# A mixture-of-experts feed-forward in two parts: tokens by chunk, then tiles of one expert pair

## The chip, the cores and the metric

The kernel runs on one core of one Trainium2 chip. The metric is the device time of one execution in microseconds (us).

## What is computed

One layer over 4 batches of 1024 tokens with 256 features (4096 tokens). `xn` is the layer norm of the input, and the output is the input plus a causal attention of `xn` plus a block of 16-head attention and feed-forward. The feed-forward, cut to what matters:

```
x = _rmsnorm(src + sa, norm1_w)
flat = x.reshape(S, C)
shared = _swiglu(flat @ W_shared_in) @ W_shared_out
g_probs = jax.nn.softmax(flat @ Wg_gate + group_bias, -1)
g_idx = jnp.argmax(g_probs, axis=-1)
...
topv, topi = jax.lax.top_k(p_expert, TOPK)
w = jnp.zeros((S, E), flat.dtype).at[jnp.arange(S)[:, None], topi].set(topv)
h = _swiglu(flat @ W1_shared)
routed = jnp.zeros_like(shared)
for e in range(E):
    routed = routed + h @ W2_experts[e] * w[:, e:e + 1]
out = x + (shared + routed).reshape(Bb, Tt, C)
return _rmsnorm(out, norm2_w)
```

There are two groups of four experts each (E = 8). A token chooses one group and two of its experts (TOPK = 2), and all experts read the same hidden activation `h` of 512 features; only their output matrices (512 x 256) differ.

## The kernel before

All is float32. A product that needs more than one pass is made from a high and a low part of each operand in three matmuls (`PASSES`: high·high, high·low, low·high). The stages are projections, causal attention, 16-head attention and the feed-forward (`feed_forward`, from 1032.8 us of the trace to its end). The feed-forward goes over 8 chunks of 512 tokens (`CH`), each of 4 tiles of 128 tokens. The order of work on each engine is written out by hand, one function per engine, and engines wait for each other by semaphores. PE fills two pairs of PSUM banks in turn (`Fills`, `f_pair`); the outputs go to four banks `f_ob`.

PE, per chunk: the attention's output projection of the next chunk (WO, L1058, 16 matmuls); eight fills of the hidden layer, each with 12 matmuls of 512 columns (L1756, four routed, four shared); after fill 5 the transposes of the next chunk's tokens (XT, 8 at L1068), after fill 6 its gates (L1082); then the experts. The tokens of a chunk have been sorted by group, so that a tile belongs to one group, except one tile where the groups meet, which is taken a second time for the other group (`f_hx`). For each of these five tiles both expert pairs of the group are multiplied: 2 x 12 matmuls of 512 columns (256 of each expert), 120 a chunk (L1764). Last come the shared outputs, 4 x 12 matmuls of 256 columns, with the transposes of the next chunk's sorted rows (XS) among them.

DVE: the product of gate and value per fill (L1888), residual, squares and normalising of the next chunk (L1123, L1131, L1132, L1139), the routing arithmetic (small instructions), the weighted sums of expert outputs (L1896, L1912 to L1920), shared sums (L1927) and the last normalising (L1939). It also inverts the softmax sums of the attention and multiplies by them (`head`, L1114, L1115). ACT: silu (L1836), high parts (L1829, L1825), squares (L1844), two square roots and one exponential per chunk, each with a change of its function table. POOL: low parts of the hidden layer (L1677, eight a chunk), copy of the meeting tile (L1686), `xn` plus causal attention (`whole_ya`, L1673), four indirect DMAs that send the rows to their sorted places in memory (L1043), and four that add the finished rows into the output (L1694). SP queues the loads and stores.

The names of buffers in the trace are those of the places that they share: `h_place` and `h_v` hold many buffers of the feed-forward, `i_saT` the projected attention and scratch of it.

## Time and profile before

| | |
|---|---|
| time, median of 3 runs | 1583.39 us (1582.5 to 1584.44) |
| the profiled execution: time | 1580.62 us |
| its span | 1578.8 us |
| mean granted clock of PE | 0.964 of full |
| feed-forward, PE's first matmul to the end | 1032.77 to 1578.8 us |
| one chunk in the middle | 65.1 us |
| PE busy in that chunk | 63.42 us |

The span is the time from the first to the last record, 1.8 us less than the execution's own time, which is 2.8 us under the median. A line of a timeline gives the start, the length, the engine and line, the operation with its output and inputs, the count, and in brackets how long the engine sat idle before it and what released it.

### The profile page before, as it was taken

What the parts mean: (1) busy time and instruction counts of PE and PEld (TensorE: products, weight loads), DVE (VectorE), ACT (ScalarE), POOL (GpSimd) and SP (SyncE); (2) the same over time, 40 slices, a digit from 0 to 9 for tenths busy, and PEclk for the clock granted to TensorE, in tenths of its full rate; (3) what the DMA queues carried; (4) which work ended last, traced back from release to release, by engine and by line L of the source; (5) the groups of instructions that cost most, each with busy time, mean ns of one, the idle gap of its engine ahead of it and who ended that gap; (6) DMA issues with size and microseconds to landing.
All of it is one profiled execution on the core that took longest, in us unless ns stands there. A gap on an engine that the chain in (4) does not pass through costs nothing. (4 is left out here: it accounts for less than half of the span.)

```text
span 1578.8 us, 25397 instructions
## 1 busy us (share of the span) xinstructions
PE 1454.6 (92%) x9648; PEld 852.5 (54%) x9648; DVE 1203.6 (76%) x1733; ACT 839.3 (53%) x1507; POOL 368.2 (23%) x314
## 2 busy tenths in 40 slices
PE   7998799779999999999999999769999999999994
PEld 4565577523333333333333333358787887878873
DVE  3776766699999999999999996447677676776532
ACT  2454344118888888888888888621413314123130
POOL 0435902243320000000000000022325244252441
PEclk9999899859999999999999999889999999999997
DMA  6799766331543343433333311032031230321211
GB/s 200 272 319 347 258 185 141 70 82 48 102 89 62 61 62 62 62 62 62 56 62 62 63 55 37 26 101 80 18 106 33 76 97 18 102 42 41 55 14 14
DMA packets 105845, 146.12 MB, mean 93 GB/s; under 512 B 24048, under 2 KB 74624, under 8 KB 105728
## 3 DMA queue, kind: packets, MB, share of 16 engines
q1 hardware_dynamic: 84480, 107.13, 26.7%
q0 software_dynamic: 10784, 23.76, 6.9%
q10 hardware_dynamic: 10464, 13.64, 2.8%
q8 instruction: 78, 1.28, 0.4%
q14 instruction: 39, 0.32, 0.1%
HBM read 80.90 MB, written 63.06 MB: 91 GB/s over the span
## 5 line engine op out<-in xcount | busy, mean ns | idle before, releaser
L1541 DVE TENSOR_REDUCE i_saT<-h_sq 128x2 f32<-128x1024 f32 x512 | 621.9, 1224 | 34.4 <-PE h_sq L1418 22.1
L1507 ACT ACTIVATE h_p<-h_sk 128x512 f32<-128x512 f32 x999 | 543.3, 595 | 143.9 <-PE h_sk L1439 121.6
L1460 PE MATMUL h_po<-h_p,h_v 128*32 128x256 f32 (+1 forms) x3840 | 324.3, 410 | 7.4 <-ACT h_o L1514 4.8
L1439 PE MATMUL h_sk<-h_q,h_k 50*128 50x512 f32 x999 | 255.1, 501 | 16.6 <-ACT h_p L1507 16.0
L1418 PE MATMUL h_sq<-h_k,h_q 48*128 48x512 f32 x1024 | 222.3, 429 | 20.9 <-DVE i_saT L1541 17.0
L1439 PEld LDWEIGHTS h_sk<-h_q,h_k 50*128 50x128 f32 x999 | 95.5, 185 | 241.6 <-ACT h_p L1507 232.4
L1764 PE MATMUL f_ob<-w_experts,f_h 128*128 x768 | 179.1, 392 | 0.0
L1460 PEld LDWEIGHTS h_po<-h_p,h_v 128*32 128x32 f32 x3840 | 75.8, 108 | 181.7 <-issue 85.1
L1764 PEld LDWEIGHTS f_ob<-w_experts,f_h 128*128 128x128 f32 x768 | 143.7, 188 | 31.3
L1677 POOL TENSOR_TENSOR f_h<-h_place,f_h 128x512 fp32r<-128x512 f32 x64 | 83.9, 1317 | 288.5 <-ACT f_h L1829 288.5
L1825 ACT ACTIVATE f_x1p<-f_pair 128x1024 fp32r<-128x1024 f32 x8 | 8.2, 1026 | 225.5 <-PE f_pair L1068 225.5
L1418 PEld LDWEIGHTS h_sq<-h_k,h_q 48*128 48x128 f32 x1024 | 102.3, 196 | 43.1 <-DVE i_saT L1541 38.7
L1339 POOL COPY h_v<-h_values 128x512 f32<-128x512 f32 x14 | 8.6, 612 | 474.0 <-DMA h_values<-vh_d 447.0
L1836 ACT ACTIVATE h_place<-f_pair 128x512 f32<-128x512 f32 x64 | 38.3, 598 | 126.6 <-PE f_pair L1756 124.9
L1756 PE MATMUL f_pair<-f_x1p,w_routed 128*128 128x512 f32 x384 | 93.5, 402 | 5.8 <-DVE h_place L1123 5.4
L1756 PE MATMUL f_pair<-f_x1p,w_shared 128*128 128x512 f32 x384 | 95.3, 400 | 2.1 <-DVE h_place L1888 2.1
L1888 DVE TENSOR_TENSOR h_place<-h_place,f_pair 128x512 f32<-128x512 f32 x64 | 43.3, 685 | 66.8 <-ACT h_place L1836 61.6
L1756 PEld LDWEIGHTS f_pair<-f_x1p,w_routed 128*128 128x128 f32 x384 | 72.9, 190 | 23.6 <-issue 6.2
L1896 DVE SCALAR_TENSOR_TENSOR h_place<-f_ob,h_v,h_place 128x256 f32<-128x256 f32 x128 | 61.8, 483 | 30.7 <-PE f_ob L1764 25.7
L1756 PEld LDWEIGHTS f_pair<-f_x1p,w_shared 128*128 128x128 f32 x384 | 70.4, 188 | 20.2 <-DVE h_place L1888 4.9
L746 PE MATMUL a_out<-a_v,a_pT 128*128 128x256 f32 x432 | 65.5, 305 | 7.1 <-DVE a_v L827 7.1
L719 PE MATMUL a_sc<-c_kT,c_qT 128*128 128x512 f32 (+3 forms) x192 | 68.1, 492 | 2.3 <-PEq L288 2.3
(211 smaller groups left out, 1734.3 us busy)
## 6 DMA issues: line engine op xcount, KB each, us to landing
h_q<-q_d SPq DMA_DIRECT2D x84, 128.0 KB, 5.8
h_k<-k_d SPq DMA_DIRECT2D x84, 128.0 KB, 6.7
ot_d<-h_o ACTq DMA_DIRECT2D x32, 256.0 KB, 3.3
q_d<-t_parts SPq DMA_DIRECT2D x12, 512.0 KB, 4.9
k_d<-t_parts SPq DMA_DIRECT2D x12, 512.0 KB, 5.1
h_place<-xs_d SPq DMA_DIRECT2D x8, 530.0 KB, 4.2
p_xin<-in_L_attn_x SPq DMA_DIRECT2D x8, 512.0 KB, 5.0
xn_d<-p_xn SPq DMA_DIRECT2D x8, 512.0 KB, 4.8
```

Source lines behind the costliest of these rows:

```text
L719: ins = nc.tensor.matmul(sc[u % 2][:, c:c + w], qT[b % 2][:, k, i * P:(i + 1) * P], kT[b % 2][:, k, c:c + w], start=k == 0, stop=k == KD - 1)
L746: ins = nc.tensor.matmul(out[u % 2][:, 0:D], pT[u % 2][left][:, j, :], vp[b % 2][right][:, j, :], start=j == 0 and n == 0, stop=j == i and ...
L1418: ins = nc.tensor.matmul(sq[slot % 2][:, g, :], q6[r][at, p, i * P:(i + 1) * P], k6[r][at, p, half * CH:(half + 1) * CH], start=True, stop ...
L1439: ins = nc.tensor.matmul(spread_banks[bank_at(f + g)], k6[r][at, p, j * P:(j + 1) * P], q6[r][at, p, c * CH:(c + 1) * CH], start=True, sto ...
L1460: ins = nc.tensor.matmul(po[h * VW:(h + 1) * VW, at], vh[n % RING][:, j, h, :], probs[u % PR][:, h, at], start=j == 0 and part == 0, stop= ...
L1507: nc.scalar.activation(probs[u % PR][:, h, :], spread_banks[bank_at(f)], ACT.Exp, scale=DH ** -0.5).then_inc(exp_done, 1)
L1541: nc.vector.tensor_reduce(halfmax[n % 2][:, m, :], sq[slot % 2][:, :, :], AX.X, ALU.max)\
L1677: nc.gpsimd.tensor_tensor(h[LO][:, f, :], whole[f % 2], h[HI][:, f, :].bitcast(F32), ALU.subtract).then_inc(h_split, 1)
L1756: ins = nc.tensor.matmul(ps[:, half, :], w[a][:, k, at:at + P], x1p[b][:, k, :], start=n == 0, stop=n == len(terms) - 1)
L1764: ins = nc.tensor.matmul(to, lhs(left, i), weight(right, i), start=n == 0, stop=n == len(terms) - 1)
L1888: nc.vector.tensor_tensor(whole[f % 2], sil[f % 2], fills.buffer(key)[:, 1, :], ALU.mult)\
L1896: ins = nc.vector.scalar_tensor_tensor(xs[c % 2][:, j, 0:D], ob[b][:, i * D:(i + 1) * D], wm[:, j, 2 * g + i:2 * g + i + 1], xs[c % 2][:, ...
```

## The change

The feed-forward is split into two parts. Everything up to the hidden layer stays in chunks; the expert products move behind all chunks.

**Part one**, per chunk: eight fills. Four of them are routed, now with 128 tokens as the stationary operand, so that their result has the tokens on the partitions and is written by DVE straight into a row buffer (`rows`, fills 0, 1, 2 and 7); four are shared (fills 3 to 6). After fill 1 stand the token ranks and WO, after fill 5 the transposes, after fill 7 the gates, then the shared outputs (the 48 matmuls of before). A row of a token has 1026 numbers: hidden activation (512), base (normalised token plus shared output, 256), rest (causal attention plus `xn`, 256), and two shares. SP stores the rows in memory (`rows_d`, and the hidden part also in `hidden_d`). Tokens aren't sorted by moving rows any more: there are 12 classes (group and pair of experts), DVE computes each token's place in its class's list (`classify`, `weigh`, `place`), and POOL scatters the 4-byte token number to it (L1097). `x1p` is split from the chunk's own transposed tokens, so the transposes of sorted rows (XS) fall away, as do the meeting tile, the four accumulating DMAs and the per-chunk last normalising. The inversion of softmax sums is made once per batch on a small tile, and the inverses are loaded spread over the features (`load_inverses`), so `head` is two multiplications of 512 columns without a reciprocal.

In the last chunk DVE works out where each class's tiles begin and which experts they need (`locate`, `pick`), and POOL fetches the lists.

**Part two**: 43 tiles (32 full ones' worth and up to 11 more, since each class ends in a part-filled tile), each of up to 128 tokens of one class. POOL gathers a tile's rows (128 x 1026 numbers) six tiles ahead; PE transposes the hidden part (4 transposes) and multiplies with the two experts of the class (24 matmuls of 256 columns, with the expert's number loaded from memory on the chip); ACT makes high part, square and root; DVE low part, two weighted sums, and the last normalising and addition; POOL scatters the finished rows to the output. The hidden parts of the first four tiles are gathered earlier, from `hidden_d`.

Constants, the sending of token numbers and `head`:

```diff
+CLASSES = 2 * (EPG * (EPG - 1) // 2)
+TILES = N // P + CLASSES - 1
+TABLE = TILES + 1
+BASE, REST, SHARES = HID, HID + D, HID + 2 * D
+ROW = SHARES + 2
...
-            pool.indirect_dma_start(self.xs_d, bass.IndirectOffsetOnAxis(self.sent_to[c % 2][:, j:j + 1], 0),
-                                    self.x1[:, j, :], None).then_inc(self.sent, 16)
...
+            pool.indirect_dma_start(places, bass.IndirectOffsetOnAxis(self.sent_to[c % 2][:, j:j + 1], 0),
+                                    self.tokens[:, c * TPC + j:c * TPC + j + 1], None).then_inc(self.sent[c % 2], 16)
...
-        if q == 0:
-            dve.wait_ge(self.values_in, (c + 1) * Chunk.VALUES)
-        at = (slice(None), q // 2, slice(q % 2 * (CH // 2), (q % 2 + 1) * (CH // 2)))
-        self.link(dve, self.nc.vector.reciprocal(tot[at], tot[at]))
-        self.nc.vector.tensor_tensor(saT[at], val[at], tot[at], ALU.mult).then_inc(self.sa_done, 1)
+        dve.wait_ge(self.values_in, (c + 1) * Chunk.VALUES)
+        for m in range(KD):
+            self.nc.vector.tensor_tensor(saT[:, m, :], val[:, m, :], tot[:, m, :], ALU.mult).then_inc(self.sa_done, 1)
```

POOL's order, and SP's stores:

```diff
                     if c:
-                        add(c - 1)
-                    if c + 1 < NCH:
-                        routing.send(pool, c + 1)
+                        routing.send(pool, c)
+                    if c < LASTS:
                         whole_ya(c + 1)
-                add(NCH - 1)
-                pool.wait_ge(added, NCH * TPC * 16)
+                    else:
+                        routing.gather_lists(pool)
+                    for i in range(KH):
+                        low_parts(c, i)
...
+                for t in range(EARLY):
+                    gather_early(t)
+                pool.wait_ge(rows_stored, NCH * 16)
+                AHEAD = SLOTS - 2
+                for t in range(AHEAD):
+                    gather(t)
+                for t in range(TILES):
+                    scatter(t)
+                    if t + AHEAD < TILES:
+                        gather(t + AHEAD)
...
+                def store_hidden(c):
+                    wait.ge(*fills.released((SLOTS_OF_CHUNK - 1, c)))
+                    given = rows[c % 2][:, :, 0:HID]
+                    sp.dma_start(tokens(hidden_d, c), given).then_inc(hidden_stored[c % 2], 16)
+                    sp.dma_start(tokens(rows_d, c)[:, :, 0:HID], given).then_inc(hidden_stored[c % 2], 16)
```

PE:

```diff
-                            ins = nc.tensor.matmul(ps[:, half, :], w[a][:, k, at:at + P], x1p[b][:, k, :],
-                                                   start=n == 0, stop=n == len(terms) - 1)
+                            if f in TILE_OF:
+                                left = x1p[b][:, k, TILE_OF[f] * P:(TILE_OF[f] + 1) * P]
+                                right = ffw.routed[a][:, k, half * HID:(half + 1) * HID]
+                            else:
+                                at = half * HID + PIECE_OF[f] * P
+                                left, right = ffw.shared[a][:, k, at:at + P], x1p[b][:, k, :]
+                            ins = nc.tensor.matmul(ps[:, half, :], left, right, start=n == 0, stop=n == len(terms) - 1)
...
-                        lhs = (lambda part, i: h[part][:, i, j * P:(j + 1) * P]) if j < TPC else \
-                            (lambda part, i: hx[part][:, i, :])
-                        at = slice(first + 2 * g, first + 2 * g + 2) if j == TPC else bass.ds(first + 2 * g, 2)
-                        output(c, k, ob[b][:, :], lhs, lambda part, i: w2s[part][:, at, i, :])
...
+                def turn_tile(t):
+                    key = ("TILE", t)
+                    if t < EARLY:
+                        pe.wait_ge(early_in[t], 16)
+                    else:
+                        pe.wait_ge(row_in[t % SLOTS], (t // SLOTS + 1) * 16)
+                    pe.wait_ge(*fills.emptied(key))
+                    given = early[t] if t < EARLY else slot(t)
+                    for i in range(KH):
+                        ins = nc.tensor.transpose(fills.buffer(key)[:, 0, i * P:(i + 1) * P],
+                                                  given[:, i * P:(i + 1) * P], ident)
+                    ins.then_inc(fills.made, 1)
+                def experts(t):
+                    b, used = bank(SHARED_OUTS + t)
+                    both = [pe.value_load(picks[0:1, i, t:t + 1], min_val=0, max_val=E - 1) for i in range(2)]
+                    pe.wait_ge(tile_free[b], used)
+                    pe.wait_ge(*fills.released(("TILE", t)))
+                    for i, e in enumerate(both):
+                        ins = output(ob[b][:, i * D:(i + 1) * D],
+                                     lambda part, k: h[part][:, t % KH, k * P:(k + 1) * P],
+                                     lambda part, k: w2s[part][:, bass.ds(e, 1), k, :])
+                    ins.then_inc(tile_made, 1)
...
                     for j in range(TPC):
-                        experts(c, j, groups[j] * EPG)
-                        if j == 0 and more:
-                            routing.count(pe, c + 1, fills)
-                    experts(c, TPC, EPG)
-                    for j in range(TPC):
                         shared(c, j)
-                        if j == 1 and more:
-                            turn_sorted(c + 1)
+                pe.wait_ge(routing.picked, 1)
+                turn_tile(0)
+                for t in range(TILES):
+                    if t + 1 < TILES:
+                        turn_tile(t + 1)
+                    experts(t)
```

ACT and DVE:

```diff
+                        if f in PIECE_OF:
+                            first_part(c, PIECE_OF[f], f)
+                        if f == ROOT_AT and more:
+                            routing.root(act, c + 1)
...
+                tile_high(0)
+                for t in range(TILES + 2):
+                    if 2 <= t:
+                        root(t - 2)
+                    if t + 1 < TILES:
+                        tile_high(t + 1)
+                    if 1 <= t <= TILES:
+                        square(t - 1)
...
+                    if f in TILE_OF:
+                        if f == 0 and c >= 2:
+                            dve.wait_ge(hidden_stored[c % 2], c // 2 * 2 * 16)
+                        to = rows[c % 2][:, TILE_OF[f], 0:HID]
+                    else:
+                        n = c * KH + PIECE_OF[f]
+                        if n >= 2:
+                            dve.wait_ge(h_split, n - 1)
+                        to = whole[PIECE_OF[f] % 2]
+                    nc.vector.tensor_tensor(to, sil[f % 2], fills.buffer(key)[:, 1, :], ALU.mult)\
                         .then_inc(fills.free_of(key), 1)
...
+                def final(t):
+                    at = slice(t % KEPT, t % KEPT + 1)
+                    dve.wait_ge(sd2_done, t + 1)
+                    link(nc.vector.reciprocal(rstd2[:, at], sd2[:, at]))
+                    link(nc.vector.scalar_tensor_tensor(base(t), base(t), rstd2[:, at], n2[:, :], ALU.mult, ALU.mult))
+                    nc.vector.tensor_tensor(base(t), base(t), slot(t)[:, REST:REST + D], ALU.add).then_inc(fin_done, 1)
...
+                tile_low(0)
+                for t in range(TILES + 2):
+                    if t + 1 < TILES:
+                        tile_low(t + 1)
+                    if 1 <= t <= TILES:
+                        sums(t - 1)
+                    if 2 <= t:
+                        final(t - 2)
+                    if 1 <= t <= TILES:
+                        mean_square(t - 1)
```

**How the order moves.** Three places, each with the rows of before and then of after.

DVE in the middle of a chunk, from the first fills to the normalising of the next chunk. L1131 to L1133 are its squares, L1137 and L1139 its normalising, L1888 a fill's product. Before:

```order
L1131 TENSOR_TENSOR i_saT<-h_place 128x1024
L1132 TENSOR_REDUCE h_v<-i_saT 128x4 [waits p_x_in1]
L1133 TENSOR_SCALAR h_v<-h_v 128x4 [waits p_x_in1]
L1888 TENSOR_TENSOR h_place<-h_place,f_pair 128x512 [waits p_sd_done1,p_made10]
L1932 TENSOR_SCALAR h_v<-h_v 128x4 [waits p_made40]
L1888 TENSOR_TENSOR h_place<-h_place,f_pair 128x512 [waits p_sd_done1,p_made01]
L1137 RECIPROCAL h_v<-h_v 128x4 [waits t_sw_done0]
L1139 SCALAR_TENSOR_TENSOR h_place<-h_place,h_v,w_n 128x256 [waits p_x_in1]
L1139 SCALAR_TENSOR_TENSOR h_place<-h_place,h_v,w_n 128x256 x3
```

After, L1197 is the residual, L1205 to L1207 the squares, L1212 and L1214 the normalising, L2089 a fill's product:

```order
L1197 TENSOR_TENSOR h_place<-f_pair,i_xn 128x1024 [waits t_values_stored0,a_rows_in0,p_made01]
L2089 TENSOR_TENSOR f_rows<-h_v,f_pair 128x512 [waits p_made60,a_rows_in1]
L1205 TENSOR_TENSOR i_saT<-h_place 128x1024
L1206 TENSOR_REDUCE h_v<-i_saT 128x4 [waits p_made01]
L1207 TENSOR_SCALAR h_v<-h_v 128x4 [waits p_made01]
L2089 TENSOR_TENSOR h_place<-h_v,f_pair 128x512 [waits p_made51,p_made61]
L2089 TENSOR_TENSOR h_place<-h_v,f_pair 128x512 [waits p_made51,p_made60]
L1212 RECIPROCAL h_v<-h_v 128x4 [waits p_tables,p_made31]
L1214 SCALAR_TENSOR_TENSOR h_place<-h_place,h_v,w_n 128x256 [waits p_made01]
L1214 SCALAR_TENSOR_TENSOR h_place<-h_place,h_v,w_n 128x256 x3
L2089 TENSOR_TENSOR h_place<-h_v,f_pair 128x512 [waits p_made51,p_made61]
```

The residual moves from ahead of the first fill to behind the second, and the normalising from behind the product of the third fill (of eight) to behind that of the fifth.

POOL over one chunk. Before, from the copy of the meeting tile on:

```order
L1686 ISA [waits p_sd_done1]
L1686 COPY f_hx<-f_h 128x512
L1686 REGISTER_ALU
L1686 COPY f_hx<-f_h 128x512
L1677 TENSOR_TENSOR f_h<-h_place,f_h 128x512 [waits p_sd_done0] x4
L1694 DMA out_dram<-h_place,r_tokens 4096x256 [waits p_var_done0,p_made51,p_x_in0]
L1694 DMA out_dram<-h_place,r_tokens 4096x256 x3
L1043 DMA xs_d<-h_place,r_sent_to 4096x265 [waits t_values_stored1]
L1043 DMA xs_d<-h_place,r_sent_to 4096x265 x3
L1673 TENSOR_TENSOR h_place<-h_place,i_xn 128x1024 [waits p_xn_done0,t_rot_done1]
L1677 TENSOR_TENSOR f_h<-h_place,f_h 128x512 [waits p_sd_done0] x4
```

After, a whole chunk, and the start of the next:

```order
L1097 DMA idx_d<-h_v,r_sent_to 49280x1 [waits p_xn_done1]
L1097 DMA idx_d<-h_v,r_sent_to 49280x1 x3
L1822 TENSOR_TENSOR h_place<-h_place,i_xn 128x4x256 [waits p_made10,t_values_stored0]
L1826 TENSOR_TENSOR f_h<-h_place,f_h 128x512 [waits p_made50] x4
L1097 DMA idx_d<-h_v,r_sent_to 49280x1 [waits p_xn_done1]
L1097 DMA idx_d<-h_v,r_sent_to 49280x1 x3
L1822 TENSOR_TENSOR f_rows<-f_rows,i_xn 128x4x256 [waits p_made10,t_values_stored0]
L1826 TENSOR_TENSOR f_h<-h_place,f_h 128x512 [waits p_made50] x4
```

The four sends, now of token numbers (L1097), and `whole_ya` (L1822) stand ahead of the chunk's four low parts (L1826), where they stood behind all eight (L1677); L1694 and L1686 are gone from the chunk.

DVE at the end of the program. Before, the last chunk's extra sums of the meeting tile, the shared sums and the last normalising:

```order
L1914 SCALAR_TENSOR_TENSOR h_values<-f_ob,h_v,h_values 128x256 [waits p_made11,p_made30]
L1914 SCALAR_TENSOR_TENSOR h_values<-f_ob,h_v,h_values 128x256 [waits p_x_in1]
L1920 SCALAR_TENSOR_TENSOR h_place<-h_values,h_v,h_place 128x256 [waits p_made31]
L1920 SCALAR_TENSOR_TENSOR h_place<-h_values,h_v,h_place 128x256 x3
L1927 TENSOR_TENSOR h_place<-f_ob,h_place 128x256 [waits p_made11,p_x_in1]
L1927 TENSOR_TENSOR h_place<-f_ob,h_place 128x256 [waits p_made11] x3
L1932 TENSOR_SCALAR h_v<-h_v 128x4 [waits p_made40]
L1937 RECIPROCAL h_v<-h_v 128x4 [waits p_made50]
L1939 SCALAR_TENSOR_TENSOR h_place<-h_place,h_v,w_n 128x256 [waits p_x_in1]
L1939 SCALAR_TENSOR_TENSOR h_place<-h_place,h_v,w_n 128x256 x3
```

After, one tile of part two, which comes 43 times:

```order
L2102 TENSOR_TENSOR f_h<-f_pair,f_h 128x512 [waits p_st_xn0]
L2110 SCALAR_TENSOR_TENSOR f_rows<-f_ob,f_rows 128x256 [waits p_lo_done1,p_taken00]
L2110 SCALAR_TENSOR_TENSOR f_rows<-f_ob,f_rows 128x256 [waits p_made01]
L2126 RECIPROCAL f_rstd<-f_sd 128x1 [waits p_st_xnT1]
L2127 SCALAR_TENSOR_TENSOR f_rows<-f_rows,f_rstd,w_n 128x256 [waits p_made01]
L2128 TENSOR_TENSOR f_rows<-f_rows 128x256 [waits p_made01]
L2120 TENSOR_SCALAR f_ms<-f_ss 128x1 [waits p_st_xn1]
```

A tile has seven instructions: the low part of the tile after (L2102), the two sums of the tile before (L2110), the normalising and addition of the one before that (L2126 to L2128), and the mean square (L2120).

## Rows read from the trace of the kernel before

**Rows 1.** The page: busy time of each engine over the span, share, instructions.

```profile
PE 1454.6 (92%) x9648; PEld 852.5 (54%) x9648; DVE 1203.6 (76%) x1733; ACT 839.3 (53%) x1507; POOL 368.2 (23%) x314
```

**Rows 2.** Windows: us, busy of PE, PEld, DVE, ACT, POOL, clock, DMA, GB/s.

```profile
1107.10:1172.20 65.10, 63.42 (x318) 53.09 (x317) 47.45 (x102) 17.79 (x32) 24.74 (x19) 1.00 0.25 64
1044.80:1048.20 3.40, 2.95 (x7) 2.40 (x8) 0.90 (x6) 0.00 (x0) 0.00 (x0) 0.50 0.37 123
```

**Rows 3.** Timeline of PE, one chunk: start, length, line, operation, count, idle before.

```profile
1107.13 3.62 PE L1058 MATMUL f_pair<-w_out,i_saT 128*128 128x256 f32 x16
1110.39 11.54 PE L1756 MATMUL f_pair<-f_x1p,w_routed 128*128 128x512 f32 x48
...
1129.33 1.06 PE L1068 MATMUL f_pair<-h_v,h_place 128*128 128x128 f32 x8 [1.68 <-DVE h_place L1888]
...
1133.02 1.85 PE L1082 MATMUL f_pair<-w_gate,i_saT 128*128 128x10 f32 x16
...
1137.61 5.67 PE L1764 MATMUL f_ob<-w_experts,f_h 128*128 x24
...
1165.67 2.99 PE L1764 MATMUL f_ob<-w_shared_out,f_h 128*128 128x256 f32 x24
```

**Rows 4.** Groups by line and shape, 1080 to 1579 us: busy us, mean ns.

```profile
L1677 POOL TENSOR_TENSOR f_h<-h_place,f_h 128x512 fp32r<-128x512 f32 x56 | 73.7, 1321 | 262.3 <-ACT f_h L1829 262.3
L1896 DVE SCALAR_TENSOR_TENSOR h_place<-f_ob,h_v,h_place 128x256 f32<-128x256 f32 x127 | 61.3, 483 | 30.7 <-PE f_ob L1764 25.7 <-issue 1.7
L1888 DVE TENSOR_TENSOR h_place<-h_place,f_pair 128x512 f32<-128x512 f32 x56 | 37.8, 684 | 53.7 <-ACT h_place L1836 49.8 <-issue 3.2
L1836 ACT ACTIVATE h_place<-f_pair 128x512 f32<-128x512 f32 x56 | 33.5, 598 | 109.3 <-PE f_pair L1756 107.6 <-ACT h_place L1844 1.6
L1043 POOL DMA_INDIRECT xs_d<-h_place,r_sent_to x28 | 28.2, 1006 | 13.8 <-issue 8.2 <-DVE r_sent_to L1209 5.6
L1673 POOL TENSOR_TENSOR h_place<-h_place,i_xn 128x1024 f32<-128x1024 f32 x7 | 16.9, 2417 | 0.2
L1131 DVE TENSOR_TENSOR i_saT<-h_place 128x1024 f32<-128x1024 f32 x6 | 7.3, 1219 | 0.0
```

**Rows 5.** Timelines of DVE and POOL around 1190 us.

```profile
1187.13 1.68 DVE L1139 SCALAR_TENSOR_TENSOR h_place<-h_place,h_v,w_n 128x256 f32<-128x256 f32 x4
...
1189.74 3.93 DVE L1939 SCALAR_TENSOR_TENSOR h_place<-h_place,h_v,w_n 128x256 f32<-128x256 f32 x4
...
1191.05 1.56 POOL L1677 TENSOR_TENSOR f_h<-h_place,f_h 128x512 fp32r<-128x512 f32 x1 [0.27 <-ACT f_h L1829]
```

**Rows 6.** Timeline of ACT around a change of its function table.

```profile
1120.31 1.28 ACT L1098 ACT_TABLE_LOAD   x1
1121.60 0.20 ACT L1098 ACTIVATE h_v<-h_v 128x4 f32<-128x4 f32 x1
...
1121.92 1.28 ACT L1836 ACT_TABLE_LOAD   x1
```

**Rows 7.** PE's sequencer: loads of the group numbers, and address arithmetic of expert matmuls.

```profile
L1803 PEldq TENSOR_LOAD <-r_picks x4: 296/298/305, 1495.5 to 1497.5; - x4
...
L1764 PEldq FUSED_REGOPS  x4: 46/48/65, 1134.8 to 1135.7; - x4
```

**Rows 8.** DMA issues: KB of each, median us from issue to landing.

```profile
i_xn<-in_L_ffn_W_experts POOLq DMA_DIRECT2D x8, 512.0 KB, 4.2
...
i_xn<-xn_d SPq DMA_DIRECT2D x8, 512.0 KB, 6.4
```

**Rows 9.** Both ends of the stage: DVE, PE at its start, POOL at its end.

```profile
1031.28 0.42 DVE L1115 TENSOR_TENSOR i_saT<-i_val,i_tot 128x256 f32<-128x256 f32 x1
...
1032.77 6.25 PE L1058 MATMUL f_pair<-w_out,i_saT 128*128 128x256 f32 x16 [10.56 <-PEq L62]
...
1045.25 12.77 PE L1756 MATMUL f_pair<-f_x1p,w_routed 128*128 128x512 f32 x48 [5.36 <-DVE h_place L1123]
...
1568.63 1.55 POOL L1694 DMA_INDIRECT out_dram<-h_place,r_tokens  x1 [0.30 <-issue]
```

825 lines of the change are left out of this document (458 added, 367 removed).

## The prediction

> **What bounds the kernel now.** I read the page's busy shares first: PE is busy 92% of the span [rows 1]. Then the stage that changes: a window over one feed-forward chunk shows 65.10 us with PE busy 63.42, DVE 47.45, ACT 17.79, POOL 24.74, at clock 1.00 [rows 2]. The timeline of PE over this chunk [rows 3] has one gap, 1.68 us at the transposes. So PE sets the end, and its own list is the budget: WO 3.45 (3.26 to the next start, 3.62 to its own end); a fill of 12 matmuls 2.85 (four took 11.54, of which some 0.15 overlaps what follows); transposes 0.87 (1.06 with such an overlap); gates 1.69 (1.85 likewise); the 120 expert matmuls 27.7 (1137.61 to 1165.67, less 0.36 for the ranks); shared outputs 5.8 (24 in 2.99 less the overlap, 0.121 per matmul of 256 columns, against 0.231 for 512).
>
> **What PE no longer does.** Experts: 8 x 27.7 = 222 us go. The second part has 43 tiles x 24 = 1032 matmuls of 256 columns, 125 us, and 172 transposes, 19 us. With XS gone (8 x 0.87), that would be 85 us less. The question is how much of it dependencies return, since the cover of 27.7 us of expert matmuls also leaves the chunks. I rebuild the time from stage to stage.
>
> **Start.** DVE's inversions of chunk 1 end the stage before at 1031.7 [rows 9]; the feed-forward starts at 1031.9 now, 0.9 earlier than PE's 1032.8, as only POOL's sends and their landing are left there. The first fill waits for ACT's high parts (1.02) and DVE's low parts (1.22): 2.3. After such an idle time the clock is at half (1.2 of 2.4 GHz): the window 1044.80 to 1048.20 shows 0.50 after 5.36 us of idle PE [rows 2, 9]. What that costs: four fills took 12.77 there against 11.54 (+1.2), and WO after 10.56 idle took 6.25 against 3.62 (+2.6) [rows 9, 3]. Here +2.8, since a fill is longer than WO was and so is the idle time. Sum 5.1.
>
> **A chunk of part one.** PE's own work is 8 x 2.85 + ranks 0.5 (an estimate from the gates' small matmuls, 0.11 each, with more columns) + WO 3.45 + 0.87 + 1.69 + 5.8 = 35.1. The order of DVE shows a chain that is longer. It runs round once per chunk, and no work of PE lies beside some of it:
> - WO 3.45, fill 2 2.85, its silu and product 1.35 (0.60 and 0.68 [rows 4] and handovers);
> - squares 1.22 + 1.22 + 0.17 = 2.6 [rows 4]. They stand beside POOL's `whole_ya` (2.42 [rows 4]), which comes 5.2 after the place numbers (four sends of 1.0 and 0.3). DVE and POOL hinder each other: four normalising instructions took 1.68 alone and 3.93 with POOL's low parts beside them [rows 5]. I take 1.2 here, the lower half of what `whole_ya` can cost;
> - product of fill 3 0.7; then ACT in order: high part 0.62, table 1.28, root 0.20, table 1.28, silu 0.60 [rows 6], with handovers 4.1; product of fill 4 0.7, which stands ahead of the normalising on DVE;
> - normalising 1.9 (reciprocal 0.18 and 1.68 [rows 5]), with one POOL low part (1.32 [rows 4]) beside it +1.3; transposes 0.87;
> - fills 6 and 7 5.7, gates 1.69, shared outputs 5.8, fills 0 and 1 of the next chunk 5.7, silu and product 1.4, handovers 0.3, and WO again.
>
> Sum 41.6. Seen from PE: 35.1 of work, 0.9 idle ahead of WO, some 5.3 ahead of the transposes (before: 1.68), 0.4 elsewhere. Without the collisions it would be 39.1, and with both at their full price 42.8. Seven chunks less 1.7 (the first has no ranks and no sends): 289.5. `head` costs no PE time: two multiplications (0.68 each) stand behind the product of fill 5, where DVE waits for the transposes anyway; if it did not wait, they would be 1.4 per chunk on the chain. The same holds for `classify` (22 small instructions of some 0.2, 4.4 us): it lies beside the shared outputs (5.8) and fills 0 and 1, and ends before the ranks are wanted.
>
> **The clock.** An idle time of 5.36 let it fall [rows 2, 9], one of 1.68 did not [rows 2, 3]. An idle time of 5.3 per chunk is just at the first of these. I take a dip at the transposes with +1.7 per chunk, between the prices above (1.2 and 2.6), 7 x 1.7 = 11.9; bounds 0 and 7 x 2.6 = 18.
>
> **Last chunk.** 22.8 fills, 0.5 ranks, 5.8 shared, and 3.3 in which `locate` and `pick` (some 18 instructions on DVE, up to 528 numbers wide) delay products: 32.4. The list's round trip through memory is beside the last fills.
>
> **Change-over.** PE has nothing between the last shared output and the first transposed tile. The last fill's product (1.4) releases two stores of 1 MB; transfers of 0.5 MB landed after 4.2 to 6.4 [rows 8], so 8 to 9 for both; then an indirect gather (1.0 to 1.55 issue [rows 4, 9], some 2 landing), transposes 0.44, high part 0.6, low part 0.7. Less the shared outputs beside it (5.8): 9.9 idle, and 3 for half a clock after it: 12.9. Bounds 8 and 18.
>
> **A tile of part two.** Four loops compete, and the longest sets the pitch:
> - DVE with ACT: DVE's seven instructions are 0.69 + 0.48 + 0.48 + 0.17 + 0.48 + 0.42 + 0.16 = 2.88 ([rows 4] for the wide ones), with gaps 3.07. The mean square releases ACT's root (0.20), behind which in ACT's order stands the next high part (0.60), for which DVE's next low part waits. With handovers 3.98. The square (0.6) is beside the final steps.
> - PE: 24 x 0.121 + 0.44 = 3.35; its sequencer: eight groups of address arithmetic at 0.30 (four from 1134.8 to 1135.7) and two loads at 0.66 (four from 1495.5 to 1497.5) [rows 7], at most 3.9.
> - POOL: a scatter and a gather, 1.0 to 1.55 each with 0.3 between [rows 4, 9]: 2.6 to 3.7.
> - The rows: the low part of tile t+1 stands ahead of the final steps of t-2 on DVE, those release scatter t-2 and then gather t+4. So a row's arrival releases the row three tiles later: 0.44 + 0.6 + 0.7 + 1.0 + 1.1 + 2.9 on POOL = 6.7 and the landing of 525 KB, over three tiles. Landings were 4.2 to 6.4 [rows 8]; at 4.2 it is 3.6 per tile, at 6.4 it is 4.4.
>
> I take 4.0 per tile, nearest to the DVE and ACT loop, whose durations are all in rows: 42 x 4.0 + 2.9 = 170.9. Bounds 3.9 and 4.4: -4 and +17. The Trainium skill ("DMA: Bandwidth & Descriptors", anatomy of one DMA on the software path) gives some 2.0 us and the bytes over 436 GB/s; an estimate by it is a landing of 3.2 us, below every row of this size here, and the loop of the rows would be 3.3. That would change nothing in the sum.
>
> **End.** Last tile: sums 1.0, square 0.6, mean square, root, final 1.4, then two scatters 3.7: 6.7. Behind the last issue of POOL the span ran on by 8.6 (1568.63 + 1.55 to 1578.8) [rows 9, 1]; kept.
>
> **Sum.** 1031.9 + 5.1 + 289.5 + 11.9 + 32.4 + 12.9 + 170.9 + 6.7 + 8.6 = 1569.9 of span, +1.8 = 1571.7 against 1580.62 of the profiled execution, -9. That execution lay 2.8 under the median, so the forecast is **1574** against 1583.39.
>
> **Rivals.**
> *A, the rows bound the tiles (slower).* Gathers of 128 rows of 4 KB land later than contiguous loads, since rows lie anywhere and each gather has a scatter beside it. It decides from a landing of 3 x 4.0 - 6.7 = 5.3 on. At 7, 4.6 per tile: +25, 1600. For it: 6.4 for a load among others. Against: 4.2 for one as large, and a light DMA load (share 0.25 [rows 2], with little else in part two). 0.15.
> *B, chunks run more smoothly.* The clock never falls and POOL's work misses DVE's: -11.9 - 7 x 2.5 = -29, 1545. For it: 5.3 is at the edge, and both collisions hang on about a microsecond. Against: POOL's low part is released by the very high part that precedes the root. 0.20.
> *C, changes of the function table cost more than their record.* Rows 6 show the load (1.28) and the next ACTIVATE 0.01 behind its end, so 4.1 above. In this change two loads lie on the chain of each of seven chunks where PE covered them before; with a stall as long as the load behind each, it would be 2 x 1.28 x 7 = 18 more, 1592. The Trainium skill ("ScalarE: Activation LUTs", what ACT_TABLE_LOAD costs) has such a rule: some 1380 ns of drain beside the 1283 of the load, 2.66 us for each switch. The trace agrees with the load and shows no such drain behind it. 0.07.
> *E, tiles stay at half clock.* PE's small gaps in each tile keep it at 0.50 after the change-over: 6.7 per tile, +116, 1690. Against: at half speed PE would be the longest loop and so busy without a gap, and the four fills that took only 1.2 longer had their clock back on the way [rows 9, 3]. 0.05.
> Something else, such as a wait that I don't see: 0.05.
>
> **How the numbers follow.** The forecast case has 0.48, with a range of its own of 1560 to 1590 (tiles 3.9 to 4.2, dips 0 to 18, change-over 8 to 18). A measurement can tell this kernel's time from no change by about 0.2%, 3.2 us: faster is under 1580.2, slower over 1586.6. Of the 0.48, 0.33 are faster, 0.09 the same, 0.06 slower. With B 0.20: faster 0.53. A, C, E and most of the rest: slower 0.37. Same 0.10. The range from 1545 to 1605 takes in A, B and C and leaves out E and the far ends.
>
> **What would show it.** In the trace of after: chunk pitch 41.6 with 5.3 idle at the transposes, released by the normalising; a granted clock under 1.00 in the windows just behind; tile pitch 4.0, where PE waits for DVE's low part and DVE for ACT's high part; a change-over of 10 us idle. A pitch of 39 is B; a PE that waits in the tiles for gathers is A; a gap between table load and ACTIVATE is C. The forecast is wrong if the tile pitch leaves 3.9 to 4.4, each tenth of a microsecond being 4.2 us.

## The result, and the profile after

The changed kernel takes **1617.91 us** (median of 4 runs, 1616.16 to 1618.15) against 1582.95 of the kernel before (4 runs, 1582.2 to 1584.44): a ratio of 1.0194, 95% interval 1.0162 to 1.0226. It is slower by 35 us. The forecast was 1574, its range ended at 1605, and its sign was wrong. The profiled execution took 1618.15 with a span of 1616.3, against a forecast span of 1569.9: 46.4 are missed.

The page of after begins with the busy time of each engine over the span (compare [rows 1]), and its section on DMA issues has the size of each and the median us from issue to landing (compare [rows 8]):

```profile
PE 1412.5 (87%) x9829; PEld 829.3 (51%) x9829; DVE 1143.3 (71%) x1786; ACT 859.9 (53%) x1573; POOL 356.5 (22%) x356
PEclk9999899758999999999999999579989999979998
rows_d<-h_place SPq DMA_DIRECT2D x4, 1028.0 KB, 16.8
rows_d<-f_rows SPq DMA_DIRECT2D x4, 1028.0 KB, 16.7
rows_d<-h_place SPq DMA_DIRECT2D x4, 1024.0 KB, 17.1
rows_d<-f_rows SPq DMA_DIRECT2D x4, 1024.0 KB, 14.8
hidden_d<-h_place SPq DMA_DIRECT2D x4, 1024.0 KB, 8.0
idx_d<-h_v,r_sent_to POOLq DMA_INDIRECT x32, 8.4
h_place<-rows_d,r_listed POOLq DMA_INDIRECT x23, 4.3
```

PE has 42 us less to do, as planned, and is busy 87% in place of 92%: it waits more than it saved. The last number of each issue line is the time to landing and tells where: a megabyte of rows lands after 15 to 17 us, where stores of the same size to `hidden_d` take 8.0 and 6.3, and the four scatters of 4-byte numbers for a chunk have a median of 8.4 (over all chunks). PE's timeline from the end of the attention to the transposes of the second and third chunk (compare [rows 3, 9]):

```profile
1035.07 1.94 PE L1596 MATMUL h_po<-h_p,h_v 128*32 128x512 f32 x8
1064.03 7.99 PE L1942 MATMUL f_pair<-w_routed,f_x1p 128*128 128x512 f32 x24 [27.02 <-DVE f_x1p L2074]
...
1091.24 1.97 PE L1128 MATMUL f_pair<-h_v,f_rows 128*128 128x128 f32 x8 [4.54 <-DVE f_rows L1214]
...
1114.70 3.69 PE L1116 MATMUL f_pair<-w_out,i_saT 128*128 128x256 f32 x16 [1.18 <-DVE f_rows L2089]
...
1132.43 1.09 PE L1128 MATMUL f_pair<-h_v,h_place 128*128 128x128 f32 x8 [2.89 <-DVE h_place L1214]
1137.33 4.50 PE L1942 MATMUL f_pair<-f_x1p,w_shared 128*128 128x512 f32 x12 [3.80 <-DVE h_place L2089]
```

The first line is the attention's last matmul, the second the feed-forward's first fill: 27.02 idle. Set against the forecast, stage by stage:

| | forecast | after | difference |
|---|---|---|---|
| attention's last matmul ends | 1022.2 | 1037.0 | +14.8 |
| idle until the first fill | 12.0 | 27.0 | +15.0 |
| chunks 0 to 6 (with dips and half clock at first) | 304.2 | 313.2 | +9.0 |
| last chunk | 32.4 | 38.5 | +6.1 |
| change-over to the first expert | 12.9 | 19.2 | +6.3 |
| 43 tiles | 170.9 | 165.2 | -5.7 |
| end | 15.3 | 16.1 | +0.8 |

The forecast's marks are its own: first fill at 1031.9 + 2.3 = 1034.2, chunks 2.8 + 289.5 + 11.9, end 6.7 + 8.6. The differences add up to the 46.4, but for rounding. In the kernel before, the attention's last matmul ended at 1022.2 and its feed-forward ran from 1032.77 to 1578.8, 546.0; that of after runs from 1064.03 to 1616.3, 552.3. So of the 37.5 us between the two spans, 6.2 are in the feed-forward and 31.3 lie ahead of it: 14.8 in the attention and 16.5 in the idle time between.

**The idle time.** POOL's timeline there, then windows (us, busy time and count of PE, PEld, DVE, ACT and POOL, granted clock, DMA share, GB/s), then SP and ACT:

```profile
1037.25 1.47 POOL L1097 DMA_INDIRECT idx_d<-h_v,r_sent_to  x1 [91.24 <-DVE r_sent_to L1319]
...
1041.57 0.96 POOL L1097 DMA_INDIRECT idx_d<-h_v,r_sent_to  x1 [0.30 <-issue]
```

```profile
1048.00:1052.00 4.00, 0.00 (x0) 0.00 (x0) 0.00 (x0) 0.00 (x0) 0.00 (x0) 0.50 0.00 0
```

```profile
1061.63 0.36 SPq L1879 DMA_DIRECT2D h_place<-ya_d  x1
```

From 1044 to 1061 no engine works and the DMA engines show a share of 0.00. The four sends (`send`, the scatters of token numbers) landed 7.1, 11.6, 14.7 and 16.9 us after their issue, the last at 1058.5, by the semaphore that POOL waits for. The packets recorded for them end by 1043.3, so the trace doesn't show what holds the landing for 15 us more. Behind the wait POOL has a DRAIN of 2.1 (1058.69 to 1060.79), then the barrier between the stages opens, SP queues its first load of the next stage 3.1 after the landing, and ACT's high parts follow.

**Inside a chunk.** SP and POOL around the second transposes; POOL's operation on two lines is `whole_ya` (L1822) and low parts (L1826):

```profile
1128.16 0.36 SPq L1879 DMA_DIRECT2D h_place<-ya_d  x1
```

```profile
1133.09 2.17 POOL L1822 TENSOR_TENSOR h_place<-h_place,i_xn 128x1024 f32<-128x1024 f32 x1 [12.43 <-DMA h_place<-ya_d]
1135.22 2.48 POOL L1826 TENSOR_TENSOR f_h<-h_place,f_h 128x512 fp32r<-128x512 f32 x2
```

```profile
1113.00:1116.00 3.00, 1.82 (x11) 1.58 (x10) 1.67 (x7) 0.60 (x1) 0.12 (x1) 1.00 0.95 71
```

The row buffer holds the attention's part `ya` for the chunk after next, so SP may load it only once the rows have been stored. The stores take 16.7, with the DMA engines at a share of 0.95 while only 71 GB/s move. The load comes at 1128.16, `whole_ya` waits 12.43 on POOL for it, the low parts of the hidden layer stand behind it in POOL's order, and DVE's next product behind those: that is PE's new wait of 3.80 for fill 6. Three of the seven chunks have this wait (3.80, 4.58 and 2.94); the other four have a longer one at the transposes, up to 6.82. In the three longest of these (5.80, 5.80 and 6.82) the late `whole_ya` and low parts stand beside DVE's normalising, which takes 4.8, 4.8 and 5.6 in place of 1.67. DVE's line and POOL's line in the longest:

```profile
1355.44 5.61 DVE L1214 SCALAR_TENSOR_TENSOR f_rows<-h_place,h_v,w_n 128x256 f32<-128x256 f32 x4
1355.58 2.37 POOL L1822 TENSOR_TENSOR f_rows<-f_rows,i_xn 128x1024 f32<-128x1024 f32 x1 [10.18 <-DMA f_rows<-ya_d]
```

Both waits together are 44.1 us in the seven chunks; the forecast had 7 x 5.3 = 37.1.

### The profile page after: what moved, and what is told of

It is laid out like the page before. It is cut to its first block and busy times, and to the rows that moved or that the text cites. A ratio compares the mean times of both kernels' runs of the same rounds, so it can differ in the third digit from the quotient of the medians.

```text
span 1616.3 us, 26408 instructions
## 1 busy us (share of the span) xinstructions
PE 1412.5 (87%) x9829; PEld 829.3 (51%) x9829; DVE 1143.3 (71%) x1786; ACT 859.9 (53%) x1573; POOL 356.5 (22%) x356
## 5 line engine op out<-in xcount | busy, mean ns | idle before, releaser
L1677 DVE TENSOR_REDUCE i_saT<-h_sq 128x2 f32<-128x1024 f32 x512 | 621.9, 1223 | 39.7 <-PE h_sq L1554 27.5
L1554 PE MATMUL h_sq<-h_k,h_q 48*128 48x512 f32 x1024 | 223.6, 432 | 20.6 <-DVE i_saT L1677 16.8
L1949 PE MATMUL f_ob<-w_experts,f_h 128*128 x1032 | 136.5, 289 | 10.6 <-issue 9.0
L1949 PEld LDWEIGHTS f_ob<-w_experts,f_h 128*128 128x128 f32 x1032 | 127.8, 193 | 18.8 <-issue 18.8
L2025 ACT ACTIVATE h_v<-f_pair 128x512 f32<-128x512 f32 x64 | 38.1, 595 | 178.3 <-PE f_pair L1942 178.2
L1942 PE MATMUL f_pair<-w_routed,f_x1p 128*128 128x512 f32 x384 | 98.4, 411 | 29.7 <-DVE f_x1p L2074 27.0
L2089 DVE TENSOR_TENSOR h_place<-h_v,f_pair 128x512 f32<-128x512 f32 x48 | 32.9, 685 | 94.5 <-ACT h_v L2025 76.6
L1942 PEld LDWEIGHTS f_pair<-w_routed,f_x1p 128*128 128x128 f32 x384 | 74.7, 197 | 47.9 <-DVE f_x1p L2074 28.8
L1942 PEld LDWEIGHTS f_pair<-f_x1p,w_shared 128*128 128x128 f32 x384 | 80.3, 212 | 33.9 <-DVE h_place L2089 14.5
L2102 DVE TENSOR_TENSOR f_h<-f_pair,f_h 128x512 fp32r<-128x512 f32 x43 | 29.7, 692 | 68.2 <-ACT f_h L2031 68.2
L1097 POOL DMA_INDIRECT idx_d<-h_v,r_sent_to x32 | 31.4, 982 | 204.2 <-DVE r_sent_to L1319 196.9
L306 POOL TENSOR_TENSOR h_spare<-h_spare,t_sin 128x512 f32<-128x512 f32 x28 | 42.0, 1533 | 101.2 <-DVE h_spare L182 101.2
## 6 DMA issues: line engine op xcount, KB each, us to landing
rows_d<-h_place SPq DMA_DIRECT2D x4, 1028.0 KB, 16.8
rows_d<-f_rows SPq DMA_DIRECT2D x4, 1028.0 KB, 16.7
```

The costliest lines, as they stand in the source:

```text
L306: last = nc.gpsimd.tensor_tensor(swap[:, j, :], swap[:, j, :], sin[:, s, :], ALU.mult)
L1554: ins = nc.tensor.matmul(sq[slot % 2][:, g, :], q6[r][at, p, i * P:(i + 1) * P], k6[r][at, p, half * CH:(half + 1) * CH], start=True, stop ...
L1677: nc.vector.tensor_reduce(halfmax[n % 2][:, m, :], sq[slot % 2][:, :, :], AX.X, ALU.max)\
L1942: ins = nc.tensor.matmul(ps[:, half, :], left, right, start=n == 0, stop=n == len(terms) - 1)
L1949: ins = nc.tensor.matmul(to, lhs(left, i), weight(right, i), start=n == 0, stop=n == len(terms) - 1)
L2025: nc.scalar.activation(sil[f % 2], fills.buffer(key)[:, 0, :], ACT.Silu).then_inc(sil_done[f % 2], 1)
```

## Experiments

In the later runs the kernel before itself spread more (medians 1591.9, 1591.6 and 1585.3 in three groups, single runs 1578 to 1604). Its only profile is the one shown first; in those of the changed kernels the attention ends anywhere from 1027 to 1053 us, with stretches at half clock of different length. Ratios are against the kernel before in the same group of runs, stages are read from one profile for each kernel, and they are compared from the first fill on. That part took 552.3, 553.5 and 553.1 in three kernels that are the same there.

### Is it the wait for the sends?

The changed kernel was timed again, and once without the stage's last wait:

```diff
                 routing.send(pool, 0)
-                pool.wait_ge(routing.sent[0], Routing.SENDS)
```

> The changed kernel itself, beside the kernel before on the chip of these runs, for a ratio to hold the others against. 1.019 as on the first chip; the time between the first fill and the end of the span 550 to 553 us, and 26 to 28 us of idle PE in front of it, whatever the granted clock does in the attention stage.

> The changed kernel without POOL's wait, at the end of the attention stage, for the four scatters of chunk 0's token numbers. Theory (the landing of the 4-byte scatters holds the barrier in front of the feed-forward): the 19.1 us between the last issue and SP's first load shrink to some 2, the first fill moves from 1064.0 to about 1046 to 1048, and the whole is 16 to 18 us shorter (about 1601). Rival (something else holds the barrier, such as the store of the attention's last output or the loads of inverses): first fill within 2 us of 1064, time 1616 to 1619. Second rival (the scatters still hold up what POOL or its DMA queue does next, so the gain is given back in the first chunk): first fill early, but the start of chunk 1 less than 8 us earlier.

The repetition of the changed kernel gave 1624.09, ratio 1.0227 (1.0162 to 1.0293), first fill to end 553.5, just over what was expected. Without the wait: ratio 1.0165 (1.0074 to 1.0257), 1608 to 1623 us, first fill to end 553.1, and PE's idle time is still there:

```profile
1054.81 5.55 PE L1941 MATMUL f_pair<-w_routed,f_x1p 128*128 128x512 f32 x13 [26.58 <-DVE f_x1p L2073]
```

In the trace POOL's DRAIN at the barrier, 7.6 us long in the kernel before, takes 20.8 in the place of the wait: 1030.8 to 1051.6, where the last scatter landed at 1050.6, 16.8 after its issue. So here the barrier waits for POOL's transfers without a semaphore too. The time did not clearly change; the rival that named this outcome put it down to something other than the scatters, which the next experiment rules out. In the kernel before the DRAIN ended at 1030.5 and DVE's inversions at 1031.7, so there the inversions came last, as the prediction read it.

### Sends of chunk 0 behind the barrier

```diff
                 routing.constants(pool)
-                routing.send(pool, 0)
-                pool.wait_ge(routing.sent[0], Routing.SENDS)
...
                 for c in range(NCH):
-                    if c:
-                        routing.send(pool, c)
+                    routing.send(pool, c)
```

> The changed kernel with chunk 0's four scatters of token numbers issued in the feed-forward, behind the first whole_ya, instead of at the end of the attention stage. After the run without the wait, POOL's drain at the end of the stage took 20.8 us in its place, so the scatters themselves hold the barrier. Theory: without them PE's idle time between the stages falls from 26.6 to 27.7 us to 7 to 10 (store of the last attention output 2, barrier 1, high and low parts 2.3), and the time is 16 to 20 us shorter; the scatters land while chunk 0 is computed and hold nobody. Rival (the long barrier has another cause, as the first run could still be read): idle time over 20, time unchanged. Rival on the other side: the scatters now delay the loads and stores of chunk 0, and its end comes less than 10 us earlier.

1603.26, ratio 1.0091 (1.0053 to 1.0129). PE's timeline:

```profile
1033.62 8.11 PE L1939 MATMUL f_pair<-w_routed,f_x1p 128*128 128x512 f32 x24 [6.21 <-DVE f_x1p L2071]
...
1072.53 4.60 PE L1939 MATMUL f_pair<-w_routed,f_x1p 128*128 128x512 f32 x12 [4.68 <-DVE h_place L1223]
```

The idle time falls from 27.0 to 6.2: the sends are its cause. But chunk 0 now takes 50.8 in place of 43.4, the second line being one of its new waits. A third of the gain (7.4 of 20.8) is given back. DVE's line ahead of that wait:

```profile
1070.05 1.29 DVE L1191 TENSOR_TENSOR i_saT<-i_val,i_tot 128x512 f32<-128x512 f32 x2 [7.13 <-DMA i_tot<-rt_d]
```

`rt_d` holds the inverted softmax sums. Their store is only 64 KB and is issued at 1043.27, while the last of the four sends is being issued; it lands after 20.2 us. In the changed kernel it is issued 15 us after the sends have landed and takes 7.4. So here the loads of the inverses are queued only at 1063.50, and `head` on DVE is late. Whether the sends hold this store is not shown: other loads run beside it too.

### What makes a 4-byte scatter slow?

Two kernels send chunk 0's numbers later, as above, and scatter four probes at the end of the attention, for which POOL waits. In the first the four have rows of 256 bytes, of 64 bytes, of 4 bytes at places 64 bytes apart, and of 4 bytes at neighbouring places; in the second all four have 4 bytes, 64 bytes apart:

```diff
+    def probe(self, pool):
+        pool.wait_ge(self.placed, 1)
+        for j, to in enumerate(self.probes):
...
+            pool.indirect_dma_start(to, bass.IndirectOffsetOnAxis(at, 0), self.x1[:, j, 0:n], None).then_inc(self.probed, 16)
+        pool.wait_ge(self.probed, 4 * 16)
```

> As the run with later scatters, and four other scatters of 128 rows each at the end of the attention stage, with a wait for them: 256 bytes a row, 64 bytes a row, 4 bytes at places 64 bytes apart, 4 bytes at the dense places of the changed kernel, in this order in one queue. In the changed kernel four dense 4-byte scatters landed 7.1, 11.6, 14.7 and 16.9 us behind their issues, one every 4.5 us. If neighbouring 4-byte places in one line of memory are slow (one write waits for the other): the first three land within 2 to 4 us of their issue and only the dense one adds 4 to 5. If the small payload is slow: 256 bytes fast, both 4-byte ones add 4 to 5 each. If it is the count of rows, whatever their size: 4 to 5 for each of the four, and PE's idle time between the stages is 26 to 28.

> As the run with the four probes, but all four scatters at the end of the attention stage write 4 bytes a row, at places 64 bytes apart. In the run with four kinds all had landed 4.1 us behind the last issue, one dense one among them, where four dense ones take 16.9. If it is the neighbourhood of places: landing of the last 3 to 5 us behind its issue, PE's idle time between the stages 13 to 15 us as with the probes (14.5). If it is several small scatters in one queue, wherever they write: 15 to 18 behind the issue and 26 to 28 of idle time.

```profile
1042.34 0.95 POOL L1106 DMA_INDIRECT probe_dense<-h_place,r_sent_to  x1 [0.31 <-issue]
```

```profile
1048.18 0.95 POOL L1106 DMA_INDIRECT probe_apart<-h_place,r_sent_to  x1 [0.30 <-issue]
```

With one dense scatter (the first fence, last of the four) POOL's wait ended 5.0 us after its issue, with none (the second) 2.1 us after. The last of the four dense ones of the changed kernel took 16.9. PE's idle time was 14.54 and 11.64; each kernel was executed once, in 1617.43 and 1619.06, so their times say nothing. So neither the size of 4 bytes nor the count of four is slow, but 4-byte numbers written to neighbouring places. The one dense scatter adds 2.9 us, where 4 to 5 were expected; of four, each landing is 3.5 to 6.3 us behind the one before, where their issues are 1.3 to 1.5 apart. Four scatters at places 64 bytes apart cost 11.64 - 6.21 = 5.4 of idle time, and the 12.0 of the forecast had 5.8 for them: its price is right for such places.

### `whole_ya` behind the low parts

POOL does all low parts of a chunk first, and then `whole_ya`:

```diff
-                    if c < LASTS:
-                        whole_ya(c + 1)
-                    else:
+                    if c == LASTS:
                         routing.gather_lists(pool)
                     for i in range(KH):
                         low_parts(c, i)
+                    if c < LASTS:
+                        whole_ya(c + 1)
```

> The changed kernel with POOL's addition of causal attention (whole_ya) moved behind the four low parts of a chunk. Theory (in each chunk the low parts queue behind that addition, which waits for a load that waits for the stores of rows): the idle time in front of fill 6 (3.80 in the chunk at 1137) goes to under 1, the one in front of the transposes stays near 3, and the pitch of a chunk falls from 44.4 to 45 to about 41; seven chunks give 20 to 28 us (about 1594). Rival (the high part, silu and table loads on ACT set that time anyway, as my sum had it): pitch 43 to 45, time within 6 us of 1618. Rival on the other side: the addition comes so late now that the next chunk's residual waits for its load of xn: pitch over 45, time over 1620.

1614.41, ratio 1.0181 (1.0115 to 1.0248); first fill to end 545.8, 6.5 less, where 20 to 28 were expected. PE's wait for fill 6 is gone, as the order says. But two chunks have a long wait at the transposes, 12.04 and 9.19. PE's line of the first of them and DVE's ahead of it:

```profile
1177.33 1.97 PE L1128 MATMUL f_pair<-h_v,f_rows 128*128 128x128 f32 x8 [12.04 <-DVE f_rows L1214]
```

```profile
1175.39 0.18 DVE L1212 RECIPROCAL h_v<-h_v 128x4 f32<-128x4 f32 x1 [9.07 <-DMA rows_d<-f_rows]
```

DVE waits 9.07 for the store of the rows, because the normalised tokens go into the same buffer. The stores with the longest median take 20 us here. The order was one path on which the slow stores reach PE, and not the only one.

### Rows of another length

A row has 1026 numbers, 4104 bytes. One kernel has rows of 1024 numbers (the two shares aren't carried and numbers of the rest stand for them, so that part two computes with other weights), the other rows of 1056 numbers, 4224 bytes, with zeros behind the shares:

```diff
-BASE, REST, SHARES = HID, HID + D, HID + 2 * D
-ROW = SHARES + 2
+BASE, REST, SHARES = HID, HID + D, HID + D
+ROW = HID + 2 * D
```

```diff
-ROW = SHARES + 2
+USED = SHARES + 2
+ROW = 1056
...
+                for s in range(2):
+                    nc.gpsimd.memset(rows[s][:, :, USED:ROW], 0.0)
```

> The changed kernel with rows of 1024 numbers (4096 bytes) instead of 1026 (4104 bytes); left out is that the two shares travel with the row, numbers of the rest part stand for them. Same instructions on all engines but a copy of 8 numbers a chunk, 0.2% fewer bytes. Theory (runs of 2 KB that begin at odd multiples of 8 bytes make the stores slow: DMA engines 85 to 95% busy at 60 to 150 GB/s): both stores of a chunk land after 7 to 9 us instead of 15 to 21, the change-over is some 8 us shorter, POOL's addition comes earlier and chunks are 2 to 4 us shorter each, in sum 20 to 35 us (about 1590). Rival (the three stores of 3 MB share the bandwidth and are slow for that, not for their place): landings 14 to 20 as before, time within 4 us of 1618.

> The changed kernel with rows of 1056 numbers (4224 bytes, a multiple of 128), the shares kept and 30 numbers of padding written. If only a start at a multiple of 64 or 128 bytes counts: as with even rows, landings of 8 to 10 us, less 3% for bytes, about 1592. If it takes a multiple of 512 bytes: landings 13 to 20 as before, 1615 to 1622. If bytes alone count: 3% slower stores, 1619.

1593.87, ratio 1.0022 (0.9993 to 1.0051), and 1595.44, ratio 1.0037 (0.9997 to 1.0076). The stores of the second, though they carry more bytes, and then a chunk and the change-over of its PE:

```profile
rows_d<-h_place SPq DMA_DIRECT2D x4, 1088.0 KB, 4.2
rows_d<-f_rows SPq DMA_DIRECT2D x4, 1088.0 KB, 7.0
rows_d<-h_place SPq DMA_DIRECT2D x4, 1024.0 KB, 8.7
```

```profile
1275.22 5.67 PE L1946 MATMUL f_pair<-w_routed,f_x1p 128*128 128x512 f32 x24
...
1301.68 1.97 PE L1129 MATMUL f_pair<-h_v,h_place 128*128 128x128 f32 x8 [4.37 <-DVE h_place L1215]
1303.30 3.58 PE L1946 MATMUL f_pair<-f_x1p,w_shared 128*128 128x512 f32 x12
...
1316.92 5.67 PE L1946 MATMUL f_pair<-w_routed,f_x1p 128*128 128x512 f32 x24
...
1405.66 1.09 PE L1974 MATMUL f_pair<-h_v,h_place 128*128 128x128 f32 x4 [7.17 <-issue]
```

Fill 6 waits for nothing, and the chunk is 1316.92 - 1275.22 = 41.7 long, the half clock at its transposes (1.97 for 1.06) included. The seven chunks take 298.8, where the forecast had 304.2 and after has 313.2; PE's waits at transposes and fill 6 are 33.6 in them, 10.5 less than in after, and the idle time of the change-over is 7.17 in place of 16.52. From first fill to end this kernel takes 531.8, that with rows of 4096 bytes 524.0; the forecast for that part was 1569.9 - 1034.2 = 535.7, the changed kernel needs 552.3. So 20.5 us hang on how long a row is, more than half of the loss.

The Trainium skill ("DMA: Bandwidth & Descriptors", how a descriptor splits into AXI transactions) says that transactions start at multiples of 256 bytes, so a transfer that starts between them can need one more. By that page of the Trainium skill 2 KB would then need nine for eight, an estimate of 12% more transactions; of the rows of 4224 bytes half start off such a multiple and would pay too, about half as often as those of 4104. These runs show 1.7 to 4 times the landing for 4104 bytes against 4224 here. The Trainium skill ("Collectives: The Full Stack", rules for kernel authors) wants the buffers of collectives at multiples of 32 bytes, so that a write needs no reading first. These are not collectives; of the three lengths only 4104 breaks such a rule. That fits the two kernels above, and not the kernel with both and POOL's other order below, whose stores are slow with 4224; no run shows the reading itself.

### Both together, and with POOL's other order

> Rows of 1056 numbers and the later scatters together. From the first fill to the end of the span 532 us, as with these rows alone (531.8), and the first fill 17 to 20 us earlier: 36 to 40 us less than the changed kernel, so within 8 us of the kernel before, and a ratio of 0.99 to 1.00. If the two gains overlap, less than 30.

> As the last, and POOL's whole_ya behind the four low parts. Against it: the wait of 4.37 us in front of the transposes is set by ACT's and DVE's chain, as the sum had it, and not by POOL any more, so the order gives only what a collision of POOL with the squares costs, 0.5 to 1.3 us a chunk, 4 to 9 us in all. Rival: the residual waits for the later load of xn, or the normalising for the store of rows (9 to 12 us in two chunks of the order alone), 0 to 10 us longer.

Later sends and rows of 1056 numbers: 1581.77, ratio 0.9947 (0.9914 to 0.998), just faster than the kernel before. PE is idle 6.21 ahead of the first fill, and first fill to end is 537.9, 6.1 more than with the rows alone, since chunk 0 alone takes 53.2 in place of 43.2: DVE waits 10.20 there for the inverses, as above. The expectation for that part, 532, is missed by as much. With POOL's other order as well: 1585.98, ratio 0.9984 (0.9947 to 1.0021), no gain where 4 to 9 us were expected; its rival held, since two chunks wait 8.10 and 5.96 at the transposes, where DVE waits for the store of the rows. Two of its store lines:

```profile
rows_d<-h_place SPq DMA_DIRECT2D x4, 1088.0 KB, 18.3
rows_d<-f_rows SPq DMA_DIRECT2D x4, 1088.0 KB, 12.2
```

So rows of 4224 bytes can be slow too, and the length is not the only cause. In its first five chunks SP queues loads for `head` (`i_val`, `i_tot`) right ahead of these stores, and the packets of a store take 12 to 15 us; in the last three, which have no such loads, they take 2.9 to 4.7. In the last three chunks of the changed kernel, where no such loads stand ahead either, they still take 6.1 to 10.9, against 2.9 to 3.1 in the kernel with rows of 1056 numbers. So the length matters by itself, and what SP has queued ahead seems to matter beside it; no run changes that order alone, and why either slows a store stays open.

### Is the chain that the forecast names the bound?

The forecast made a chunk 41.6 long by a chain through the root and the normalising. If it holds, moving these up must shorten the chunks that wait for nothing else. First the normalising, from behind fill 4's product to behind fill 3's; then also ACT's root ahead of fill 3's high part; both on top of the later sends and the longer rows:

```diff
-                        if f == 4 and more:
+                        if f == 3 and more:
                             if c:
                                 dve.wait_ge(rows_stored, c * 16)
                             routing.normalise(dve, c + 1, normal(c + 1))
```

```diff
                         hidden(c, f)
-                        if f in PIECE_OF:
-                            first_part(c, PIECE_OF[f], f)
                         if f == ROOT_AT and more:
                             routing.root(act, c + 1)
+                        if f in PIECE_OF:
+                            first_part(c, PIECE_OF[f], f)
```

> Later scatters, rows of 1056 numbers, and DVE's normalising of the next chunk one fill earlier: behind the product of fill 3 instead of fill 4. By the chain of my sum the transposes wait for root, table load, silu and product of fill 4, and then the normalising (1.9); its new place puts the normalising beside ACT's table load and silu, so the idle time of 4.37 us ahead of the transposes falls to 2.2 to 2.8 and the pitch of a chunk by 1.5 to 2.2; seven chunks 10 to 15 us, ratio to the kernel before 0.984 to 0.989. Rival (the transposes wait for something else as well, the buffer or POOL's collision): idle time over 3.8, time as with the two changes alone, 0.995. Rival on the other side: the normalising now waits for the root ahead of the product of fill 4, and PE's fill 6 or 5 is late: over 0.997.

> As the last, and ACT takes the root ahead of the high part of fill 3 instead of behind it. The root waits for the squares on DVE, which end ahead of the product of fill 3, so its two table loads begin about 1.3 us earlier. If the chain is as in my sum: idle time ahead of the transposes 0.6 to 1.4 us less than in the last run, 4 to 9 us in all, ratio 0.979 to 0.985. Rival: the high part of fill 3 comes 2.8 us later, POOL's low part with it, and the product of fill 5 waits for that buffer: no gain, 0.985 to 0.990.

1566.82, ratio 0.9871 (0.9836 to 0.9907), and **1562.72, ratio 0.9825 (0.9781 to 0.9869)**: the second beats both kernels, the one before by 1.75%. PE's lines of the first and of the second:

```profile
1118.51 1.06 PE L1129 MATMUL f_pair<-h_v,h_place 128*128 128x128 f32 x8 [1.66 <-DVE h_place L2090]
```

```profile
1164.68 5.17 PE L1943 MATMUL f_pair<-f_x1p,w_shared 128*128 128x512 f32 x12 [5.38 <-DVE h_place L2090]
...
1179.93 5.67 PE L1943 MATMUL f_pair<-w_routed,f_x1p 128*128 128x512 f32 x24
...
1202.31 1.06 PE L1129 MATMUL f_pair<-h_v,h_place 128*128 128x128 f32 x8 [0.31 <-DVE h_place L2090]
...
1217.20 5.67 PE L1943 MATMUL f_pair<-w_routed,f_x1p 128*128 128x512 f32 x24
```

The wait at the transposes falls from 4.37 to 1.66 and to 0.31, the transposes take 1.06 in place of 1.97, as the clock no longer falls, and a chunk without another wait is 38.6 and then 1217.20 - 1179.93 = 37.3 long. From first fill to end: 524.5 and 516.1. Four of the seven chunks come to 38.6 and then to 37.3. The others still have another wait: two chunks of the last kernel wait for fill 6 (5.38 and 3.52) and take 43.6 and 41.1, where they took 41.4 and 42.0 without the two edits, and its chunk 0 takes 54.1, since PE waits 13.20 behind DVE, which waits for the inverses again:

```profile
1084.41 0.69 DVE L1192 TENSOR_TENSOR i_saT<-i_val,i_tot 128x512 f32<-128x512 f32 x1 [13.84 <-DMA i_tot<-rt_d]
```

Their store lands after 21.7 us here. So the fastest of these kernels still loses some ten microseconds in its chunk 0 (54.1 against 43.2 in the kernel with the rows of 1056 alone).

## Why the prediction was wrong

**The start: the step that failed first.** "The feed-forward starts at 1031.9 now, 0.9 earlier than PE's 1032.8, as only POOL's sends and their landing are left there." The trace of before had a wait of 10.56 there [rows 9], and I read it as the end of DVE's inversions, which was right: POOL's DRAIN ended 1.2 before them. The step that failed is what comes last once they are gone. That the sends' landing is part of the path was seen, and it was given the time of the old sends, as if a scatter of 4 bytes to neighbouring places were no dearer than one of a kilobyte. The last of the four landed after 16.9, with a DRAIN of 2.1 behind it, and the idle time was 27.0 for 12.0; with the sends behind the barrier it is 6.2, with 4-byte scatters to places 64 bytes apart 11.6.

**The attention: not foreseen, and partly open.** I left the attention at its old time. In after it ends 14.8 later. 0.9 of this is its start and 5.4 a longer stretch at half clock near 350 us. 1.2 are near 980, where PE is idle ahead of a WO (seen in all changed kernels, 1.1 to 5.7), and 7.3 are in its last step. A window over that step of after, behind it one of before:

```profile
1020.00:1028.00 8.00, 8.00 (x52) 2.75 (x55) 0.72 (x5) 4.35 (x9) 0.00 (x0) 0.56 0.00 0
```

```profile
1015.00:1020.00 5.00, 4.64 (x50) 1.63 (x50) 2.34 (x16) 4.77 (x10) 0.00 (x0) 1.00 0.00 0
```

The same matmuls run at half clock in after, without a gap. The change doesn't force this: three changed kernels with the same attention (without the wait, with later sends, and with POOL's other order) run this step at a granted clock of 1.00 and end the attention at 1027 to 1028. Why the clock falls in after isn't known. What they keep is a wait of 1.1 at the rank matmuls for `classify`, which now stands ahead of them (PE's line in the kernel without the wait):

```profile
1026.58 0.43 PE L1150 MATMUL h_sq<-h_v 128*128 128x60 f32 x2 [1.12 <-DVE h_v L1276]
```

Beside this, all changed kernels are slower against the kernel before than their stages explain. In the kernel with later sends and rows of 1056, for one, 4.4 less idle time and 8.1 less feed-forward make -12.5, and the ratio of 0.9947 is -8.4. So reckoned, the excess is 3 to 7 in seven kernels, 9.5 with the rows of 1024 numbers, and about 12 with POOL's other order and for the changed kernel itself. The stages are from one profile each and the intervals of the ratios are 5 to 15 us wide, so this hints at a cost in the attention and doesn't measure it.

**The stores of rows: a term that was missing in the chunks and too small behind them.** "Transfers of 0.5 MB landed after 4.2 to 6.4 [rows 8], so 8 to 9 for both" holds for rows of 4224 bytes in the kernel that changes the length alone (8.7 for the last store) and fails for 4104 (15 to 17). Inside the chunks I put no price on the stores: I looked at what the engines do, and not at what each buffer waits for until it may be loaded again. By the path store, load of `ya`, `whole_ya`, low parts, fill 6, and by `whole_ya` that now comes at other times beside DVE's work, the waits grew by 7.0 of the +9.0 (44.1 for 37.1); with rows of 4224 bytes they are 33.6. In the change-over the bounds of 8 and 18 for idle time and half clock together were passed by 1.2 (19.2), and with rows of 4224 bytes it is 10.2 in all, of which 7.17 idle, for 12.9 and 9.9 in the sum.

**The last chunk** took 38.5 for 32.4: three waits of 1.35, 2.33 and 1.55 beside `locate` and `pick`, and the last fill at half clock behind them (12 matmuls in 5.49). 3.3 was too little for them; no run tells them apart.

**What was right.** The chunk: 41.6 and 1.7 for the dip, 43.3 in all, were forecast; with rows of 4224 bytes the seven chunks are 41.7 to 43.9 long, 42.7 on average. That agreement is in part luck: a chunk without the dip would be some 40.4 and not 41.6, since the collisions cost less than the sum had. Beside POOL the squares take 1.70 for 1.22 and the normalising 2.68 for 1.67, 1.5 in all, and the sum had 2.5. The idle time at the transposes was to be 5.3 and is 4.37 there, 5.6 to 6.0 in two chunks. The chain is confirmed from its other end, by two edits on it that each shorten the four chunks without another wait. The clock: in after, behind waits of 4.0 and more the transposes take 1.9 to 1.97, behind 2.9 they take 1.1, so the dips were real. The edge isn't sharp: behind 2.88 they took 1.97 in the repetition, and behind 3.89 they took 1.19 with POOL's other order. With rows of 1056 numbers a dip costs 0.8 at the transposes (1.62 to the next start against 0.81) and 0.5 to 1.8 in the fill behind them (3.55 to 4.83 against 3.06), 1.8 on average, for which I had taken 1.7. The table loads, in ACT's timeline of after (compare [rows 6]):

```profile
1126.45 1.28 ACT L1163 ACT_TABLE_LOAD   x1
1127.75 0.20 ACT L1163 ACTIVATE h_v<-h_v 128x4 f32<-128x4 f32 x1
```

ACT goes on 0.02 behind the load, so rival C is out, and the trace shows no drain such as the Trainium skill ("ScalarE: Activation LUTs", what ACT_TABLE_LOAD costs) names. The tiles: 3.86 for 4.0. PE's timeline of two tiles, and the window over sixteen:

```profile
1443.82 0.60 PE L1970 MATMUL f_pair<-h_v,h_place 128*128 128x128 f32 x4
1444.18 3.08 PE L1949 MATMUL f_ob<-w_experts,f_h 128*128 x24
1447.09 0.60 PE L1970 MATMUL f_pair<-h_v,f_rows 128*128 128x128 f32 x4
```

```profile
1500.00:1560.00 60.00, 56.03 (x448) 52.42 (x446) 41.80 (x112) 20.49 (x65) 31.58 (x32) 1.00 0.56 172
```

PE follows with 3.3 per tile at the start and is busy 93% later; gathers land after 4.3, and PE waited for one only twice (1.54 and 0.58). So rivals A and E did not occur. The pitch of 3.86 is just under the forecast's own lower bound of 3.9 (3.79 to 3.93 over the changed kernels). DVE waits for ACT's high part as forecast, 1.1 each time, but PE isn't seen waiting for DVE's low part, so which of the loops sets the pitch isn't settled. B did not occur in after, whose chunks are longer than forecast; the fault lay in "a wait that I don't see", at 0.05. The second part is sound; what surrounds it, small transfers and their order, cost what it gave.

## What to carry to other kernels

When a change puts a new transfer on a path, cost it by a transfer of the same shape: bytes per row, where rows start, and how close the places lie, not by one of the same size. For every buffer, follow the round store, release, next load, and whoever stands behind that load on its engine; an engine's list of work doesn't show it. And a barrier at the end of a stage waits for POOL's transfers even where no semaphore does, so sends that nobody needs yet belong behind it, with an eye on what they delay there: here chunk 0 grew by 7.4, with a late store of 64 KB.

## What the runs showed of the hardware

- A store of 1 MB to rows of 4104 bytes landed after 15 to 17 us (20 in one kernel), with a DMA share of 0.90 to 0.95 and 71 to 112 GB/s; to rows of 4096 or 4224 bytes after 4.2 to 9.2, but in one kernel after 12.2 to 18.3 with rows of 4224. What slows it isn't settled.
- Four scatters of 128 4-byte numbers to neighbouring places landed 7.1, 11.6, 14.7 and 16.9 us after their issues, though the packets recorded for them ended by 1043.3, 15 us before the last landing; four to places 64 bytes apart were all there 2.1 us after the last issue.
- A store of 64 KB issued next to four such scatters landed after 20.2 and 21.7 us in two kernels; issued 15 us after they had landed it took 7.4. What held it stays open.
- POOL's DRAIN at a barrier lasted until its transfers had landed: 20.8 us without a semaphore's wait, to 1.0 us behind the last landing.
- A gather of 128 rows (525 KB) landed after 4.3, no later than contiguous loads of that size.
